# Attention and a gated feed-forward in one kernel: a new table of places for the work beside the matmul stream

## The reference

```python
x = x + xattn(layernorm(x), ctx, ctx, Wq, bq, Wk, bk, Wv, bv, Wo, bo)
x = x + ffn(layernorm(x), gate_w, gate_z, gate_s, up_w, up_z, up_s, down_w, down_z, down_s)
# xattn: q = Wq x + bq, k = Wk ctx + bk, v = Wv ctx + bv  (W is 64 x 64 over the middle axis)
#        8 heads of 64 columns, softmax(q k^T / 8) v, then Wo and bo
# ffn:   W = (int - zero) * scale, groups of 128 rows; H = 512, I = 1792
#        (silu(x @ gate) * (x @ up)) @ down
```

## Time and profile before

| | |
|---|---|
| runs (median of 3) | 413.63 us |
| profiled execution, span of its instructions | 411.8 us |
| TensorE / VectorE / ScalarE / GpSimd busy | 394.7 / 334.1 / 323.3 / 263.4 us |
| main loop, places 0 to 223 | 40.7 to 396.4 us |
| chain of waits, shares | TensorE 72%, VectorE 9%, DMA 7%, GpSimd 6%, issue 5% |

### The profile page before, as it was taken

The page is one execution under the profiler, slowest core; times in us unless marked ns, Lnnn a source line. Parts: engine busy times, 40 slices in busy tenths (PEclk is TensorE's granted clock), DMA queues, the critical chain, the costliest instruction groups (busy, mean ns, idle before and its releaser), DMA issues.

```text
span 411.8 us, 10204 instructions
## 1 busy us (share of the span) xinstructions
PE 394.7 (96%) x3901; PEld 310.7 (75%) x3901; DVE 334.1 (81%) x587; ACT 323.3 (79%) x534; POOL 263.4 (64%) x283
## 2 busy tenths in 40 slices
PE   7788899999999999999999999999999999999994
PEld 4666677877777778777788778777788788888872
DVE  4687549889899978899898878898996768777686
ACT  2656898779678888868689788787899899999960
POOL 5763698668975866387658656575766666665550
PEclk9999999999999999999999999999999999999999
DMA  7699999976861010432312010332201002320003
GB/s 224 234 187 267 340 269 260 266 187 147 210 209 27 2 25 27 125 124 94 100 53 78 0 27 11 104 121 86 68 30 51 0 2 76 127 78 26 0 2 102
DMA packets 40250, 44.97 MB, mean 109 GB/s; under 512 B 3810, under 2 KB 29578, under 8 KB 40202
## 3 DMA queue, kind: packets, MB, share of 16 engines
q1 hardware_dynamic: 32242, 36.87, 27.3%
q0 software_dynamic: 7456, 7.34, 11.5%
q10 hardware_dynamic: 504, 0.11, 0.1%
HBM read 35.34 MB, written 8.97 MB: 108 GB/s over the span
## 4 chain that ended last, share of the span: by engine, by line
PE 72%; DVE 9%; DMA 7%; POOL 6%; issue 5%; SPq 0%; POOLq 0%; ACT 0%; DVEq 0%
PE banks L907 22%; PE banks L909 20%; PE banks L920 10%; PE banks L921 10%; DMA wgu<-in_L_ffn_up_w 3%; DVE yT L1178 3%; PE banks L794 3%; DMA yT<-in_L_ffn_down_z 3%; PE banks L851 2%; POOL hr L512 1%; PE banks L811 1%; PE banks L840 1%; POOL t_sb L499 1%; PE banks L821 1%; PE banks L829 1%
## 5 line engine op out<-in xcount | busy, mean ns | idle before, releaser
L681 ACT ACTIVATE banks<-banks,ratio 128x512 f32<-128x512 f32 x336 | 206.9, 660 | 36.2 <-PE banks L909 26.3
L1178 DVE SCALAR_TENSOR_TENSOR yT<-banks,sd,yT 128x512 f32<-128x512 f32 x208 | 153.1, 744 | 34.3 <-PE banks L921 33.9
L907 PE MATMUL banks<-xT,wgu 128*128 128x512 f32 x448 | 180.2, 402 | 0.7 <-DVE t_sb L1163 0.4
L909 PE MATMUL banks<-xT,wgu 128*128 128x512 f32 x448 | 174.9, 390 | 0.0
L499 POOL TENSOR_TENSOR t_sb<-t_sb,u_sb 128x512 f32<-128x512 f32 x56 | 74.3, 1327 | 64.8 <-DVE t_sb L1163 64.5
L907 PEld LDWEIGHTS banks<-xT,wgu 128*128 128x128 f32 x448 | 84.0, 188 | 22.5 <-issue 1.6
L909 PEld LDWEIGHTS banks<-xT,wgu 128*128 128x128 f32 x448 | 84.2, 188 | 15.9
L920 PE MATMUL banks<-hr,wd 128*128 128x512 f32 x224 | 88.2, 394 | 1.8 <-POOL hr L512 1.6
L921 PE MATMUL banks<-hr,wd 128*128 128x512 f32 x224 | 87.3, 390 | 0.0
L512 POOL TENSOR_TENSOR hr<-t_sb,hr 128x512 fp32r<-128x512 f32 x56 | 73.6, 1314 | 5.1 <-ACT hr L703 0.7
L920 PEld LDWEIGHTS banks<-hr,wd 128*128 128x128 f32 x224 | 42.0, 188 | 13.2 <-DVE yT L1178 3.0
(11 more groups left out here) (114 smaller groups left out, 377.7 us busy)
## 6 DMA issues: line engine op xcount, KB each, us to landing
wgu<-z_out SPq DMA_DIRECT2D x14, 512.0 KB, 10.0
swap_d<-xn SPq DMA_DIRECT2D x18, 256.0 KB, 2.0
x_sb<-swap_d SPq DMA_DIRECT2D x72, 64.0 KB, 2.0
x_sb<-in_x SPq DMA_DIRECT2D x16, 256.0 KB, 5.0
out<-x_sb SPq DMA_DIRECT2D x16, 256.0 KB, 2.3
wgu<-in_L_ffn_gate_w POOLq DMA_DIRECT2D x7, 512.0 KB, 12.2
wgu<-in_L_ffn_up_w POOLq DMA_DIRECT2D x7, 512.0 KB, 9.8
wd_in<-in_L_ffn_down_w SPq DMA_DIRECT2D x7, 512.0 KB, 8.7
```

Source lines behind the costliest of these rows:

```text
L681: act.activation(banks[:, bank, :], banks[:, bank, :], ACT.Copy, scale=ratio[:, m, g, it:it + 1]).then_inc(done[n % 2], 1)
L907: pe.matmul(banks[:, bank, :], w, xT[:, c % 2, 0, g, :], start=g == 0, stop=False, skip_group_check=True)
L909: pe.matmul(banks[:, bank, :], w, xT[:, c % 2, 1, g, :], start=False, stop=True, skip_group_check=True).then_inc(full[n % 2], 1)
L1178: dve.scalar_tensor_tensor(y, bank, sd[:, it, b:b + 1], y, ALU.mult, ALU.add).then_inc(s_free, 1)
```

## The change

All tuples of places are written anew, each of the three chunks with attention has its own now, and the delays behind a burst become parameters (`SOFT`, `TAKE`): the second half of q and k is taken at the burst's own place instead of two places later, `take_a` at the burst's own place instead of one later. No instruction is added or removed. Two lines of the tables as they stand in the diff, and the core of the rest:

```diff
+    BURSTS = ((6, 9, 11, 17, 20, 23, 27, 31, 33, 39, 42, 46, 51), (1, 5, 8, 13, 17, 19, 25, 28, 31, 35, 38, 41, 43), (2, 6, 7, 13, 18, 22, 26, 29, 31, 39, 39, 40, 46))
+    SWAP_X = (((25, 35), (40, 47), (44, 51)), ((25, 30), (35, 40), (46, 50)))
+    SOFT = (1, 2, 3, 4, 4)
+    TAKE = (1, 0, 0)
...
-                                (6, 9, 12, 16, 20, 23, 27, 31, 33, 38, 42, 46, 51) if c == 0 else
-                                (1, 5, 7, 11, 17, 19, 25, 28, 30, 35, 38, 40, 43)):
...
-            for j, (q, q_take) in enumerate(((25, 31), (36, 42), (46, 52))):
+            for j, (q, q_take) in enumerate(SWAP_X[c - 1]):
...
-                if q - 1 in mix_after:
-                    take_a(mix_after[q - 1])
+                if q - TAKE[2] in mix_after:
+                    take_a(mix_after[q - TAKE[2]])
...
-                if q - 1 in qk_after:
-                    take_qk(qk_after[q - 1], 0)
-                if q - 2 in qk_after:
-                    take_qk(qk_after[q - 2], 1)
+                if q - TAKE[0] in qk_after:
+                    take_qk(qk_after[q - TAKE[0]], 0)
+                if q - TAKE[1] in qk_after:
+                    take_qk(qk_after[q - TAKE[1]], 1)
```

More of the change, by code:

```diff
@@ L67, in xattn_ffn @@
         for (kind, j), q in zip((("QK", 1), ("M", 0), ("SV", 1), ("QK", 2), ("MA", 1), ("SV", 2), ("QK", 3), ("MA", 2),
-                                 ("SV", 3), ("QK", 4), ("MA", 3), ("A", 3), ("SV", 4)),
-                                (6, 9, 12, 16, 20, 23, 27, 31, 33, 38, 42, 46, 51) if c == 0 else
-                                (1, 5, 7, 11, 17, 19, 25, 28, 30, 35, 38, 40, 43)):
+                                 ("SV", 3), ("QK", 4), ("MA", 3), ("A", 3), ("SV", 4)), BURSTS[c]):
             if t0 + j < NT:
                 burst_after[q0 + q] = (kind, t0 + j)
-        for j, at in enumerate(((0, 4, 4, 4), (8, 9, 9, 12), (17, 19, 20, 25), (29, 30, 35, 35)) if c == 0 else
-                               ((-7, -3, -2, -2), (1, 4, 5, 5), (3, 5, 6, 16), (28, 30, 30, 31))):
+        for j, at in enumerate(NORM1[c]):
             if t0 + 1 + j < NT:
@@ L79, in xattn_ffn @@
                     table[PER * c + q] = t0 + 1 + j
-        for j, at in enumerate(((21, 25, 26, 26), (33, 33, 39, 44), (43, 43, 44, 46), (47, 48, 48, 52)) if c == 0 else
-                               ((19, 19, 22, 22), (29, 30, 31, 33), (39, 40, 42, 44), (43, 45, 46, 48))):
+        for j, at in enumerate(NORM2[c]):
             for table, q in zip(norm2_at, at):
                 table[PER * c + q] = t0 + j
-        for j, q in enumerate((29, 46, 52, 53)):
+        for j, q in enumerate(TURN_X):
             if c == 0 or j == CT - 1:
@@ L93, in xattn_ffn @@
     for c in range(1, NCH):
-        for i, (q, q_add) in enumerate(((14, 19), (18, 24), (22, 29), (30, 38))):
+        for i, (q, q_add) in enumerate(SWAP_Y[c - 1]):
             swap_after[PER * c + q] = ("Y", CT * (c - 1) + i)
@@ L132, in xattn_ffn @@
     add_after = {0: 4, 1: 5, 4: 6, 7: 7, 12: 8, 21: 9, 28: 10, 31: 11, 37: 12, 38: 13}
-    sub_after = {q: divmod(k, 2) for k, q in enumerate((2, 4, 15, 16, 19, 23, 31, 32, 35, 41, 42, 45, 49, 51))}
+    sub_after = {q: divmod(k, 2) for k, q in enumerate(SUB)}
     with ExitStack() as keep:
@@ L587, in _ @@
                     norm1(norm1_at[3][q])
-                if q - 4 in sv_after:
-                    weigh(sv_after[q - 4])
+                if q - SOFT[4] in sv_after:
+                    weigh(sv_after[q - SOFT[4]])
                 if at and at[1] == NG - 1:
@@ L1278, in _ @@
                     swap(*swap_after[q])
[L1279 to L1288 removed]
+                if q - TAKE[0] in qk_after:
+                    take_qk(qk_after[q - TAKE[0]], 0)
+                if q - TAKE[1] in qk_after:
+                    take_qk(qk_after[q - TAKE[1]], 1)
+                if q - SOFT[0] in sv_after:
+                    most(sv_after[q - SOFT[0]])
+                if q - SOFT[1] in sv_after:
+                    less_max(sv_after[q - SOFT[1]])
+                if q - SOFT[3] in sv_after:
+                    invert(sv_after[q - SOFT[3]])
                 if q in res_after:
```

15 lines of the change are left out of this document (7 added, 8 removed).

## The result

The changed kernel is slower.

| session | changed | before | ratio, 95% interval |
|---|---|---|---|
| first, the one the forecast was for | 421.02 us | 413.62 us | 1.0156 [1.0125, 1.0186] |
| second | 417.4 us | 413.82 us | 1.0074 [1.0047, 1.0100] |
| third | 419.58 us | 413.41 us | 1.0149 [1.0117, 1.0182] |

What follows compares the result with a forecast made beforehand. TensorE was taken as the bound, busy 394.7 of 411.8 us, with 7.3 us winnable. Terms 0.2 - 0.4 + 1.8 + 1.0 + 0.2, plus 0.2 for pieces, gave 3.0 off 413.6: 410.7 us, range 409.2 to 412.3.

Steps and rivals of the forecast that it cites:

- Held operations: VectorE's two-SBUF-input operations meeting GpSimd: rule quoted, up to a GpSimd product's length lost each; no term in the sum.
- a collision at places 25 or 47 adds 0.6 each: Chunk 0, within the rival that the waits move (412.9 us, chance 0.21): a subtraction meeting GpSimd adds 0.6 us.
- Chunk 3: 0: Last chunk: only additions and swaps of y move, VectorE has a third of its time free; no change.
- Places 24 to 56, gain 1.8: Chunk 0: earlier normalisation of block 8 gains 0.6 us, moved statistics and subtractions 1.2.
- Start, gain 0.2: Loop start: place 6's burst begins 1.1 us sooner, but a later gate product leaves 0.2 at place 8.
- The early subtraction, loss 0.6: Chunk 0, places 10 to 20: VectorE waits for zeros landing at 58.3; loss 0.6, net cost 0.4 us.
- My rival: Chunk 0: late zeros hold the early subtraction and TensorE, 415.7 us; decides from landing 62.1; chance 0.12, including another wait.
- Chunk 1, net gain 1.0: Chunk 1: gains 0.5, 0.6 and 0.3 us, less 0.4 at places 95 to 104; bounds 0 and 2.1.
- Chunk 2, net gain 0.2: Chunk 2: gains of 0.8 us, against TensorE waiting about 0.6 for block 14's earlier copy.
- my 0.6: Chunk 2: block 14's copy at place 50 waits for its swap, costing TensorE about 0.6 us; bounds 0.3 and 1.8.
- the signs of being wrong: Chunk 1 no shorter than 94.5 us, an unnamed TensorE wait above 1 us, or place 8 near 50.4.
- the 2.3 of the rival: Four spots in chunks 0 to 2 each cost a half microsecond more: 0.7 gained, 412.9 us; chance 0.21.

Runs made afterwards that it cites:

- B: Changed kernel with three of chunk 3's four additions of y moved clear of GpSimd, swaps kept: 417.11 us, ratio 1.0077 to the kernel before.
- E: Changed kernel with chunk 2's additions of y, two swaps and block copies moved to GpSimd-idle places: 416.58 us, then 416.24 us, ratio 1.0079 to before.
- M: Changed kernel with only the tuple of weights' subtractions altered (2, 4, 13, 16, 20, 21, ...): 415.56 us, ratio 1.0037 to the kernel before.
- J: Kernel before with chunk 0's changed tables, new subtraction places, and q, k and mixing taken at the burst's place in chunk 0: 412.44 us, 0.9961.
- H: Kernel before with only block 5's first normalisation moved, to places 0, 3, 0, 5: 413.99 us, ratio 1.0008.
- D: Kernel before with block pair 1's weights' subtractions moved from places 15 and 16 to 10 and 14: 414.32 us, ratio 1.0004.
- C: Changed kernel with block 14's copy put back from place 50 to 52 of chunk 2: 417.73 us, ratio 1.0083 to the kernel before.
- G: Kernel before with additions of y and copies of swapped blocks in chunks 1 to 3 at GpSimd-free places: 416.32 us, ratio 1.0059.

## Why the prediction was wrong

*Held operations, the step that failed.* I wrote of places 24 to 56 that the work "fits unless a subtraction meets GpSimd", saw one such meeting in the earlier trace rows, quoted the rule on it, and then gave it no term of the sum: it appears as "a collision at places 25 or 47 adds 0.6 each". Instead of two meetings the 32 operations take 10.3 us more, and TensorE feels 0.9 + 0.6 + 0.4 of it in chunk 0, 1.2 in chunk 2 and 1.1 in chunk 3. "Chunk 3: 0", because "VectorE has a third of its time free", was wrong in kind: a mean says nothing of two additions within 4 us of a gate product. By B the term is 1.1 us, by E chunk 2's is 2.2 with the copy, by M places 22 to 56 hold 2.4. The rule itself, in the Trainium skill's "SBUF — State Buffer", section "Who interferes with whom", says no more than the additions at 359.12 and 361.05 show; the stops just named add up to 4.2 us, more than the 3.0 of the forecast, so a rival made of it and summed over the chunks could have come out slower than before.

*Places 24 to 56, gain 1.8.* Right, and hidden. M and J gain 1.9 us there; the changed kernel's subtractions gave back 2.4.

*Start, gain 0.2.* Mis-sized. Place 6 takes 1.59 us above its four stream matmuls, the projection's own included, in place of 2.83, and place 8 starts 9.62 us after the loop's start, before 10.72: 1.1 us gained. The gate product was not later but earlier (49.97, 8.8 us after the loop's start; 9.5 before). It varies, though: in the second session the same place took 2.63 us, as GpSimd waited longer for the zeros of its gate/up piece (5.0 us at the loop's start, 2.9 in the first). And H shows the gain given back behind it.

*The early subtraction, loss 0.6.* The zeros came at 59.2, 0.9 later than forecast (14.8 us after their issue at 44.41), and the subtraction was held for 0.9 us on top; the places cost 3.9 us, some 1.7 of them by the halved clock. My rival named this mechanism and wanted a landing at 62.1 for it to decide. The landing alone was not what decided: the second session's execution began the subtraction as late after the loop's start (18.4 us) and lost 0.4. It takes an early TensorE and the hold besides, and D has neither. So it is not the main part either: in the three sessions the loss from place 22 on was 4.1, 4.3 and 4.3 us, and 0.1 to 2.7 before it.

*Chunk 1, net gain 1.0.* The stops at places 90 and 94 lost 0.53 and 0.64, as forecast. New ones, 0.5 at place 91, 0.35 at 98 and 99, 0.5 at 106, stand behind an addition of 1.43 us at 197.12, one of 1.21 at 208.07 and a remainder of 1.29 at 223.13. Measured: 0.35 lost.

*Chunk 2, net gain 0.2.* The copy cost 0.45 (C), near my 0.6; the gain at place 146 was a loss of 1.2.

Summed from place 0 by the profile, the first session lost 6.9 us, the second 5.6, the third 4.4; the medians say 7.4, 3.6 and 6.2. The rest is the loop's start, which floats, and that a profile is one execution (418.6 us in the second session, where the median is 417.4). What makes the sessions differ stays open: the stop at place 13 fits the second and not the third.

Of the signs of being wrong that I had named all three came: chunk 1 took 94.85 us, place 146 stopped for 1.54, and place 8 began 9.6 us after the loop's start, which answers to 50.3 in the kernel before. There are slips in the working, none of which matters: 413.6 - 3.0 is 410.6, the start's chain from 45.95 adds up to 48.1, and four halves of a microsecond are 2.0, not the 2.3 of the rival.

## What to carry to other kernels

Before moving an instruction of VectorE that has two SBUF inputs, look at what GpSimd runs at that moment, and sum over all such instructions, not over the ones where TensorE already waits. Then ask what stands behind the new place: a free place ahead of a burst can cost more than a held one behind it (G). And measure a table by its stretches: here a gain of 1.9 us and a loss of 2.4 stood in the same 34 places.
